# The attention loop written as one planned order per head, the last head and its norms as one planned list, and the shared expert's loads issued ahead of the output's stores

## The reference, cut to what matters

```python
# third block: 1024 positions, 2 sequences (2048 tokens), 16 heads of 128, 8 key/value heads
q = einsum('btd,ndh->btnh', x, q_kernel); k, v = einsum('bsd,ckdh->cbskh', x, kv_kernel)
q = apply_rope(rms_norm(q, q_norm_scale)); k = apply_rope(rms_norm(k, k_norm_scale))
mask = (j <= i) & (i - j < 256)
probs = softmax(where(mask, q @ k.T * ATTN_SCALE, min))
y = einsum('btnh,nhd->btd', probs @ v, out_kernel)
x = x + _layernorm(y)                       # then _layernorm(x) feeds the fourth block

# fourth block: top 2 of 8 experts (352 wide), and a shared expert (1408 wide)
shared = (silu(x @ sh_gate_w.T) * (x @ sh_up_w.T)) @ sh_down_w.T
out = sum_e cur_e * combine_e + sigmoid(x @ shared_gate_w.T) * shared
x = x + _layernorm(out)
```

## Time and profile before

| | us |
|---|---|
| median of 3 runs | 2107.44 (2104.4 to 2107.78) |
| the profiled execution's own time | 2104.56 |
| its span, first to last instruction | 2102.8 |
| PE busy / DVE / ACT / POOL | 1973.7 / 1491.9 / 1179.2 / 755.9 |
| head 1 to 6 of the attention, each | 116.6 |
| first phase ends, second starts | about 1412 |

### The profile page before, as it was taken

One profiled execution on the slowest core, in us unless ns is written; L12 is line 12 of the kernel. 1 busy time (PEld: TensorE's weight loads), 2 busy tenths in 40 slices (PEclk: granted clock), 3 DMA queues, 4 the chain that ended last, 5 costly groups with the idle time before them and its releaser, 6 DMA issues. The chain is left out here.

```text
span 2102.8 us, 33161 instructions
## 1 busy us (share of the span) xinstructions
PE 1973.7 (94%) x10142; PEld 1663.6 (79%) x10142; DVE 1491.9 (71%) x3538; ACT 1179.2 (56%) x2962; POOL 755.9 (36%) x1072
## 2 busy tenths in 40 slices
PE   7999999989999999999999999859999999999996
PEld 6677777778788888888888888648788889987775
DVE  7788655897677676677676678875377778774664
ACT  6752221676666666666666666533376777773332
POOL 3441000575545555555545556630600000001442
PEclk9999999999999999999999999979999999999998
DMA  7343010244000000000000000122799999984552
GB/s 258 127 139 124 26 35 26 91 137 144 21 12 20 10 21 10 20 10 0 30 0 20 30 1 21 66 80 81 261 332 323 316 329 314 321 285 153 170 191 100
DMA packets 82632, 244.82 MB, mean 116 GB/s; under 512 B 10800, under 2 KB 11440, under 8 KB 80592
## 3 DMA queue, kind: packets, MB, share of 16 engines
q1 hardware_dynamic: 77376, 226.46, 31.2%
q0 software_dynamic: 5120, 16.78, 2.3%
HBM read 207.81 MB, written 45.61 MB: 121 GB/s over the span
## 5 line engine op out<-in xcount | busy, mean ns | idle before, releaser
L952 POOL TENSOR_SCALAR att_pr<-att_pr,rec_ri 128x384 f32<-128x384 f32 (+2 forms) x256 | 137.3, 549 | 245.4 <-DVE rec_ri L1446 245.4
L282 PE MATMUL l_xp<-att_w_hi,xT_hi 128*128 128x512 f32 x512 | 206.1, 403 | 18.1 <-ACT att_qkv L1991 10.5
L282 PE MATMUL l_xp<-att_w_hi,xT_lo 128*128 128x512 f32 x512 | 203.9, 398 | 0.0
L282 PE MATMUL l_xp<-att_w_lo,xT_hi 128*128 128x512 f32 x512 | 203.9, 398 | 0.0
L2020 ACT ACTIVATE att_pr<-att_pr,rec_nb,rec_r 128x384 f32<-128x384 f32 (+2 forms) x256 | 168.0, 659 | 38.1 <-DVE rec_nb L1417 38.0
L1991 ACT ACTIVATE att_qkv<-l_xp 128x512 f32<-128x512 f32 x128 | 76.3, 596 | 189.2 <-PE l_xp L282 176.1
L2924 POOL DMA_INDIRECT y<-moe_rows,moe_slotA x16 | 16.0, 1000 | 412.4 <-DMA moe_rows<-moe_lo_f 409.3
L2013 ACT ACTIVATE att_pT_hi<-l_out 128x768 fp32r<-128x768 f32 (+2 forms) x128 | 93.7, 732 | 102.5 <-PE l_t L282 101.7
L956 POOL TENSOR_TENSOR att_rot<-att_rot,att_rot 128x384 f32<-128x384 f32 x128 | 129.4, 1011 | 21.3 <-DVE att_rot L1440 21.3
L282 PEld LDWEIGHTS l_xp<-att_w_hi,xT_hi 128*128 128x128 f32 x512 | 97.1, 190 | 47.5 <-POOL att_w_lo L924 10.4
L1401 DVE TENSOR_TENSOR att_q_lo<-l_xp,att_q_hi 128x256 fp32r<-128x256 f32 x128 | 54.0, 422 | 111.2 <-ACT att_k_hi L1998 111.2
(11 more groups left out here) (326 smaller groups left out, 6649.4 us busy)
## 6 DMA issues: line engine op xcount, KB each, us to landing
y<-in_moe_rt SPq DMA_DIRECT2D x59, 704.0 KB, 6.3
y<-in_moe_rt SPq DMA_DIRECT2D x39, 768.0 KB, 6.2
moe_sraw_gu<-in_moe_sgu SPq DMA_DIRECT2D x44, 512.0 KB
moe_sraw_d<-in_moe_sd SPq DMA_DIRECT2D x44, 256.0 KB
moe_xs<-in_zeros SPq DMA_DIRECT2D x39, 256.0 KB, 7.6
moe_lo_f<-moe_xs SPq DMA_DIRECT2D x39, 256.0 KB, 6.5
moe_rows<-moe_lo_f SPq DMA_DIRECT2D x39, 256.0 KB, 6.3
att_raw_w<-in_qkv_w SPq DMA_DIRECT2D x8, 1024.0 KB, 4.7
```

The source lines that it names most:

```text
L282: mm = pe.matmul(out, lhsT, rhs, start=(i == 0), stop=(i == len(terms) - 1))
L952: pool.tensor_scalar(p, p, ri[:, j % 2, g:g + 1], 1.0, ALU.mult, ALU.mult).then_inc(sa("p"), 1)
```

## The change

Four parts.

1. The lag constants, `heads`, `norm_tile`, `turn_tiles` and the five functions `step` are gone. In their place each engine has a list of calls: the rest of head 0, a loop body for heads 1 to 6, and the rest. The body is rotated: it begins in the middle of the work on tiles 8 to 15 of the head before and ends with those of its own head in the same state. The splits of the next weights are single calls (`split_w_part`), spread over the list, instead of all at step 0.
2. Head 7, the norms and the 16 transposes are one list per engine, in which attention work, norms and transposes alternate.
3. The second norm of the block (`x_norm`, on DVE) is made on ACT (`x_norm_act`), with one more small DVE instruction for its shift (`x_shift`).
4. SP's walk over the experts' items uses `loads_first(items)`, which puts each S item in front of the C item before it; the other engines keep the old list. 

The memset of the tail of `y` covers 7 tiles instead of 6. No product, tile or buffer changes.

```diff
-V_LAG, TURN_LAG, SCORE_LAG, PT_LAG, PV_LAG, OUT_LAG = 1, 2, 3, 4, 5, 6
-LED = 12
...
-        def heads(eng, step, last_head):
-            def body(k, steps):
-                for i in steps:
...
-                    step(k, i, lagged)
-            body(0, range(LED, NT))
-            with eng.Fori(1, KVH - 1) as k:
-                body(k, range(NT))
...
@@ gpsimd
-            def step(k, i, lagged):
-                now = lagged(0)
-                if now and i == 0:
-                    w_lo_part(k)
...
+            with pool.Fori(1, KVH - 1) as k:
+                split_w_part(k, 1)
+                weigh(12, NT * k - 4)
+                split_w_part(k, 0)
+                rms(15, NT * k - 1)
+                split_v(15, NT * k - 1)
+                rope_add(15, NT * k - 1)
...
@@ vector
+            with dve.Fori(1, KVH - 1) as k:
+                row_max(12, NT * k - 4)
+                split_w(k, 2)
+                split_qk(13, NT * k - 3)
+                inverse(12, NT * k - 4)
+                split_p(11, NT * k - 5)
+                split_e(10, NT * k - 6)
+                sum_out(9, NT * k - 7, False)
+                split_w(k, 3)
...
@@ scalar
+                split_w_part(k, 0)
+                squares(15, NT * k - 1)
+                split_w_part(k, 1)
+                split_w_part(k, 2)
+                split_qk(13, NT * k - 3)
+                exps(12, NT * k - 4)
+                split_p(11, NT * k - 5)
+                split_e(10, NT * k - 6)
+                split_v(15, NT * k - 1)
+                split_qk(14, NT * k - 2)
+                split_w_part(k, 3)
...
@@ tensor
+            with pe.Fori(1, KVH - 1) as k:
+                turn_p(10, NT * k - 6)
+                project(k, 15, NT * k - 1)
+                project_out(k, 8, NT * k - 8)
+                scores(12, NT * k - 4)
+                turn(13, NT * k - 3)
+                turn_p(11, NT * k - 5)
+                weigh_v(10, NT * k - 6)
+                project_out(k, 9, NT * k - 7)
+                turn(14, NT * k - 2)
+                scores(13, NT * k - 3)
+                turn_p(12, NT * k - 4)
+                weigh_v(11, NT * k - 5)
+                project_out(k, 10, NT * k - 6)
+                project(k, 0, NT * k)
+                scores(14, NT * k - 2)
+                turn(15, NT * k - 1)
+                project(k, 1, NT * k + 1)
...
+            project(7, 15, 127)
+            scores(11, 123)
+            turn_p(9, 121)
...
+            project_out(7, 10, 122)
+            last_turn(0, 0)
+            scores(15, 127)
+            last_turn(0, 1)
+            turn_p(13, 125)
...
+            project_out(7, 15, 127)
+            last_turn(1, 3)
+            last_turn(2, 0)
...
@@ experts
+def loads_first(items):
+    out = list(items)
+    for k in range(1, len(out)):
+        if out[k][0] == "S" and out[k - 1][0] == "C":
+            out[k - 1], out[k] = out[k], out[k - 1]
+    return out
...
-            for kind, n in items:
+            for kind, n in loads_first(items):
```

More of the change, by code:

```diff
@@ L2239, in _ @@
+            norm.hi(act, 3, (1,))
+            norm.x_norm_act(act, 3, (2,))
+            norm.x_norm_act(act, 3, (3,))
+            norm.hi(act, 3, (2,))
+            norm.hi(act, 3, (3,))
         @block.tensor
@@ L2680, in _ @@
             turn_p(7, 7)
-            heads(pe, step, last_head)
+            turn(10, 10)
+            project(0, 12, 12)
+            scores(9, 9)
+            weigh_v(7, 7)
+            turn_p(8, 8)
+            project(0, 13, 13)
+            project_out(0, 6, 6)
+            turn(11, 11)
+            scores(10, 10)
+            weigh_v(8, 8)
+            turn_p(9, 9)
+            project(0, 14, 14)
+            scores(11, 11)
+            turn(12, 12)
+            project_out(0, 7, 7)
+            weigh_v(9, 9)
@@ new lines, in _ @@
+            pe.wait_ge(sa("cleared"), 1)
+            scores(12, 108)
+            turn_p(10, 106)
+            turn(13, 109)
+            turn_p(11, 107)
+            weigh_v(10, 106)
+            project_out(6, 8, 104)
+            project(6, 15, 111)
+            scores(13, 109)
+            turn_p(12, 108)
+            turn(14, 110)
+            weigh_v(11, 107)
+            project_out(6, 9, 105)
+            scores(14, 110)
+            turn(15, 111)
+            project(7, 0, 112)
+            scores(15, 111)
@@ new lines, in _ @@
+            turn_p(0, 112)
+            turn(2, 114)
+            weigh_v(15, 111)
+            project_out(6, 14, 110)
+            scores(2, 114)
+            turn_p(1, 113)
+            weigh_v(0, 112)
+            project(7, 4, 116)
+            turn(3, 115)
+            project_out(6, 15, 111)
+            turn_p(2, 114)
+            scores(3, 115)
+            weigh_v(1, 113)
+            project(7, 5, 117)
+            project_out(7, 0, 112)
+            turn(4, 116)
+            weigh_v(2, 114)
@@ new lines, in _ @@
+            turn_p(3, 115)
+            project_out(7, 1, 113)
+            scores(4, 116)
+            project(7, 6, 118)
+            turn(5, 117)
+            weigh_v(3, 115)
+            project_out(7, 2, 114)
+            project(7, 7, 119)
+            scores(5, 117)
+            turn_p(4, 116)
+            project_out(7, 3, 115)
+            turn(6, 118)
+            project(7, 8, 120)
+            scores(6, 118)
+            weigh_v(4, 116)
+            turn_p(5, 117)
+            project(7, 9, 121)
@@ new lines, in _ @@
+            turn(7, 119)
+            project_out(7, 4, 116)
+            project(7, 10, 122)
+            scores(7, 119)
+            turn_p(6, 118)
+            turn(8, 120)
+            weigh_v(5, 117)
+            project(7, 11, 123)
+            scores(8, 120)
+            turn(9, 121)
+            project_out(7, 5, 117)
+            project(7, 12, 124)
+            scores(9, 121)
+            turn_p(7, 119)
+            turn(10, 122)
+            weigh_v(6, 118)
+            project(7, 13, 125)
```

1190 lines of the change are left out of this document (1025 added, 165 removed).

## The result

The changed kernel takes 2089.74 us (median, 2085.76 to 2093.04), the kernel before in the same comparison 2107.61 (2104.4 to 2108.13): a ratio of 0.9915, 95% interval 0.9897 to 0.9932. It is faster by 0.85%, and 43 us slower than forecast, far outside the range of 2035 to 2066. The profiled execution took 2091.68 us with a span of 2089.9, 12.9 less than the one before.

A forecast was written before the change was run, and what follows sets the result against it. PE, 94% busy, was taken to bound the kernel, with DVE scarce in the last stage and a late DMA at the experts' end. 29 + 17 + 12.5 = 58.5 us off 2104.56 gave 2046, as a median 2047 us; range 2035 to 2066.

The forecast's parts named there:

- Part 1: Loop body: PE's four stalls at each of seven head boundaries go, 4.1 us per boundary, 29 us in all.
- Do they go?: Loop body: step arguing that new weights' splits end before PE asks and the other stalls go, 4.1 of 4.6 us regained.
- a margin of 1.1 us: Loop body: DVE's last weight split ends at 9.4 us, 1.1 us before PE asks after 10.5 us of work.
- a head above 115 us: Loop: sign of being wrong; heads were to take 112 to 113 us.
- The other fear of this part: Loop: further lockout of DVE's 1.35 us split behind POOL makes it 0.6 us late, 4 us less gain.
- Parts 2 and 3: Head 7, norms and transposes: DVE's busy time falls to 105.8 us, its idle time from 18 to 10, gaining 17 us.
- 115 us from the first norm to the phase's end: Last stage: sign of success, about 115 us for this stretch with DVE at 90%.
- Part 4: Experts' end: weights' loads issued ahead of stores end ACT's 2.08 us wait; 14 chunks in 118 to 119 us, gaining 12.5.
- the loop keeps its stalls elsewhere: Rival, loop: 2 us per head regained, 14 us instead of 29, so 2062 us; chance 0.16.
- The slower one: Rival, loop: DVE's last weight split behind `sum_out(9)` delays `project(0)`; at 5.5 us per head 2114 us; chance 0.04.

The follow-up runs named there:

- a_unroll_exit: Changed kernel with the loop over heads 1 to 6 written out on four engines and PE's first seven entries behind it in the body's order: 2054.59 us.
- a_xn: a_unroll_exit with the 16 second norms of the last stage back on DVE instead of ACT: 2056.41 us.
- b_unroll: The kernel before with its loop over heads 1 to 6 written out for all engines that run it: 2103.05 us.
- b_loads: The kernel before with only SP's order of the shared loads changed (`loads_first`): 2096.48 us.
- b_pad40: The kernel before with 40 empty instructions at DVE's start: 2106.99 us.
- a_exit: Changed kernel, loops kept, with PE's first seven entries behind the loop put in the order of the body's top: 2078.63 us.
- a_pad19: a_exit, hardware loops kept, with 19 empty instructions at DVE's start: 2064.38 us.

## Why the prediction was wrong

**Part 1 failed, at the step "Do they go?".** It asked whether the four stalls of the earlier trace rows go, and worked out a margin of 1.1 us in the middle of the body. That was right: they are gone, and a written-out head takes 112.1 us against the 112.5 that the numbers gave. What it did not ask is what the two ends of a body cost. The 29 us were 7 boundaries of 4.1. Measured, with the way back and the way out mended (a_unroll_exit), heads 1 to 6 take 674.6 us against 699.5, 24.9 or 4.15 each; the seventh boundary, that of head 0, lies in front of the loop and gave 0.5: PE waits there for `att_k_lo` for 0.90 us, which it did not before. In the changed kernel heads 1 to 6 take 712.3. The difference, 37.7 us, is the step's error: some 24 us for five ways back (4.9 each) and 13 for the way out (127.5 against 114.2). Together with the seventh boundary, 3.6, that is 41 us. The miss is 43 us between the medians and 45.6 between the profiled executions (2091.68 against 2046); the rest of the latter is 0.8 of the last stage and 3.5 of the experts. The prediction's own sign of being wrong, a head above 115 us, came true.

The row that could have warned was there: ACT's 0.38 us of "issue" in the earlier trace rows, right behind the branch. I took it as a small idle time. It was what showed of a fetch: ACT's queue branches at 874.93 and takes its next instruction at 877.32, 2.4 us later, while some 2 us of queued work, exponentials above all, go on. The change put a wait for PE in front of the branch, and nothing was queued any more. And the place of a body among the packets can't be read from the change at all: it moved because the code in front of the loop became 19 instructions shorter on DVE.

The other fear of this part, that DVE's split of a piece would stay at the loaded 1.35 us and come late, did not come true: it takes 0.68 to 0.79 us in the changed kernel.

**Parts 2 and 3 gave the forecast sum, in part by luck.** 17 us were forecast and 16.2 measured (185.3 to 169.1), `att_pr` stayed under 5 us, and DVE is the engine waited for. But the sum was to come half from DVE's busy time (114.3 to 105.8) and half from its idle time (18 to 10). From the start of head 7 to the experts DVE is busy

```profile
1232.50:1417.80 185.30, 147.40 (x805) 123.99 (x806) 144.80 (x450) 101.90 (x313) 99.49 (x153) 0.92 0.14 48
```

144.8 us before and 146.2 after (the row from 1244.80 in the result): the busy time did not fall, and all of the gain is idle time, 40.5 to 22.9 us. The shift was estimated at 0.1 us and takes 0.35, 5.6 us for 16. And the 96 instructions of `rope` in this stretch, unchanged in number, take 35.9 us instead of 30.3; why was not tried. The norms' move is 4.6 of the 16 by a_xn. The sign "115 us from the first norm to the phase's end" can't be compared: the first norm begins at 1281.9 before, not at 1278, and the new order has it 26 matrix instructions earlier on PE (241 against 267 from the start of head 7). By its own mark the stretch is 120.8 us to the last `xT_lo`.

**Part 4 held.** 12.5 forecast, 12.85 measured (131.25 to 118.4), 14 chunks in 118.4 us. (ACT asks for the weights at 1982.94, not 1982.84; it changes nothing.) In the whole sum less arrived, 9.0 us: the experts began 3.9 us earlier and at chunk 1942 the two kernels were level. The routed part had lost it, in waits of 0.3 to 0.7 us for loads from `moe_xs` and one stretch at a lower clock. From the first product of the experts to the `hs` split of chunk 1950 it was 532.7 us in the profiled execution of before, and 533.9 to 538.7 in the other 18 kernels, with 536.3 to 537.2 in the three of them that are made from the kernel before (b_unroll, b_loads, b_pad40); so this is a quick execution of before rather than a cost of the change. It was not tried on its own.

**The rivals.** The nearest in kind was "the loop keeps its stalls elsewhere", at 2062; none of the old stalls was kept, and the new ones cost more than the old. The slower one named DVE's split of the weights behind `sum_out(9)`, 5.5 us per head on top of the old head: PE never waits for that split, and a head is 117.0 us and not 122. No rival had a price for the branch, for want of any row that showed 5 us at a boundary.

## What to carry to other kernels

A hardware loop's way back is an operation with a price: here 2.0 to 2.7 us on ACT and on DVE, and a second gap of 1.5 to 1.9 where, by the estimate above, a packet's edge lies right behind the top, if nothing is queued or waited for at that moment. Put the branch in front of a wait that is there anyway, or write the loop out on the engines that wait, and count the instruction packets per trip before and after: a body that stays the same in length can fall over an edge because of code elsewhere. And where an order is planned on a ring, the end of one body must be read against the first entries behind the loop, engine by engine, as one list.

## What the runs showed of the hardware that I had not expected

19 instructions that do nothing, at the start of one engine's program, save 14 us (a_exit to a_pad19, 2078.6 to 2064.4). PE goes back over a body of one head without any fetch and pays 3.00 us each time when the body has two. And the same wait of some 3 us costs PE 3.6 us or 5: in the changed kernel the next 3 us ran at a granted clock of 0.54 at every way back, in a_exit three of five times at 1.00. What decides between the two was not found.
